# A chunked GRU with a spline layer behind it: side-by-side last input groups, a short first step, an earlier count, and extremes in eight parts

## What is computed

```python
gi = x @ W_ih + b_ih
gh = h @ W_hh + b_hh
r, z = sigmoid(i_r + h_r), sigmoid(i_z + h_z)
n = tanh(i_n + r * h_n)
h_new = (1 - z) * n + z * h
...
tok_min, tok_max = x_slice.min(axis=1), x_slice.max(axis=1)   # per token
tile_min = where(onehot, tok_min, inf).min(axis=1)            # per expert: the extremes
```

## Time and profile before

| | |
|---|---|
| median of 3 runs | 2472.63 us (2471.12 to 2473.9) |
| the profiled execution | 2474.04 us, its span 2472.5 us |
| PE busy | 2342.8 us (95%) |
| DVE busy | 1299.0 us (53%) |
| ACT busy | 658.0 us (27%) |
| POOL busy | 214.4 us (9%) |
| granted TensorE clock, mean | 0.970 |

### The profile page before, as it was taken

How to read it: one execution, slowest core, us unless ns; L and a number is a source line. 1 busy time by engine, 2 the same in 40 slices (tenths; PEclk the granted TensorE clock), 3 DMA queues, 4 the chain that set the end, 5 groups by cost and what they waited for, 6 DMA issues and landing times. The chain is left out here.

```text
span 2472.5 us, 83702 instructions
## 1 busy us (share of the span) xinstructions
PE 2342.8 (95%) x35300; PEld 1287.7 (52%) x35300; DVE 1299.0 (53%) x2691; ACT 658.0 (27%) x1333; POOL 214.4 (9%) x440
## 2 busy tenths in 40 slices
PE   7999999999999989999999999999999999977736
PEld 3444444444444445555666656666666666644412
DVE  4322121212122357676666655666666666888867
ACT  3200000000001133333333332333333333355530
POOL 0000000000000000000000000111111111123224
PEclk9999999999999999999999999999999999999965
DMA  7693131313132445444444443444444444478830
GB/s 238 204 336 128 52 128 50 126 52 128 51 145 103 153 148 156 143 143 131 136 136 136 136 132 103 120 113 117 119 115 116 119 119 119 114 221 233 240 86 5
DMA packets 177335, 330.61 MB, mean 134 GB/s; under 512 B 24272, under 2 KB 87168, under 8 KB 176192
## 3 DMA queue, kind: packets, MB, share of 16 engines
q1 hardware_dynamic: 145360, 267.53, 34.0%
q10 hardware_dynamic: 24192, 44.05, 4.8%
q0 software_dynamic: 7680, 17.57, 4.5%
HBM read 222.39 MB, written 156.77 MB: 153 GB/s over the span
## 5 line engine op out<-in xcount | busy, mean ns | idle before, releaser
L581 PE MATMUL banks<-w_hi,hi 128*32 128x512 f16 (+1 forms) x13824 | 613.1, 332 | 30.8 <-DVE hi L887 18.3
L581 PEld LDWEIGHTS banks<-w_hi,hi 128*32 128x32 f16 x13824 | 366.2, 98 | 256.9 <-issue 32.3
L314 DVE SCALAR_TENSOR_TENSOR out_stage<-acc,bias_row 128x512 f32<-128x512 f32 x168 | 116.0, 691 | 623.5 <-PE acc L372 623.5
L581 PE MATMUL banks<-w_lo,hi 128*32 128x512 f16 (+1 forms) x8192 | 355.4, 326 | 0.0
L581 PE MATMUL banks<-w_hi,lo 128*32 128x512 f16 (+1 forms) x8192 | 355.0, 326 | 0.0
L370 PE MATMUL acc<-w_hi,x_even 128*128 128x512 f16 x768 | 292.3, 381 | 12.7 <-DVE x_even L306 11.1
L371 PE MATMUL acc<-w_hi,x_even 128*128 128x512 f16 x768 | 292.2, 380 | 0.0
L372 PE MATMUL acc<-w_lo,x_even 128*128 128x512 f16 x768 | 292.1, 380 | 0.0
L581 PEld LDWEIGHTS banks<-w_lo,hi 128*32 128x32 f16 x8192 | 218.5, 97 | 114.9 <-issue 0.5
L581 PEld LDWEIGHTS banks<-w_hi,lo 128*32 128x32 f16 x8192 | 218.3, 97 | 114.5
L709 ACT ACTIVATE rz<-sums 128x512 f32<-128x512 f32 x176 | 110.9, 630 | 541.0 <-DVE sums L852 541.0
(11 more groups left out here) (172 smaller groups left out, 2167.0 us busy)
## 6 DMA issues: line engine op xcount, KB each, us to landing
stage<-gi_scratch SPq DMA_DIRECT2D x704, 96.0 KB
gi_scratch<-out_stage ACTq DMA_DIRECT2D x168, 256.0 KB, 2.0
stage<-sums_scratch SPq DMA_DIRECT2D x40, 512.0 KB
stage<-in_xT SPq DMA_DIRECT2D x32, 512.0 KB, 6.5
y<-in_x_rows SPq DMA_DIRECT2D x32, 512.0 KB, 4.4
hs_scratch<-h SPq DMA_DIRECT2D x128, 128.0 KB
x_keep<-hs_scratch SPq DMA_DIRECT2D x32, 512.0 KB, 3.9
y<-hs_scratch POOLq DMA_DIRECT2D x32, 512.0 KB, 8.2
```

Source lines behind the costliest of these rows:

```text
L314: nc.vector.scalar_tensor_tensor(out=out_stage[:, tb], in0=acc[e % BANKS][:], scalar=UNSCALE, in1=bias_row[:].rearrange("p q f -> p (q f)" ...
L581: last = nc.tensor.matmul(bank[q * COLS:(q + 1) * COLS, 0:b - a], state[:, s, j], w[:, j, q * QW + a:q * QW + b], start=first and j == 0, ...
```

## The change

- The last four groups of the last block made here (column block 5) go side by side: a quarter of k for each of the four, then the next quarter. After each quarter but the last PE counts `last_used`, and ACT and DVE convert that piece of W_hh. ACT stores the last group behind the last conversion. The clearing of the state moves ahead of the block.
- The first warm step (ZERO) multiplies one block of the state, which is zero, in place of eight. PE's first round of four steps is written out ahead of the loop.
- Set a's additional counts move to the last warm step, right behind its conversion (ACT) and its remainder (DVE); that iteration is written out on both.
- The first batch of extremes has 16 tiles, the second 14; the 15 instructions are in eight parts, and the first batch's stand in tiles 18 to 21, two in each. PE's code of these tiles is cut accordingly.

```diff
 DIFF_TILE = DIFF_FROM // 2
 
 
-EARLY = DIFF_TILE - 4
+EARLY = DIFF_TILE - 6
 ENDS_TILES = ((0, EARLY), (EARLY, TILES - 2), (TILES - 2, TILES))
 ENDS_STEPS = 15
 ENDS_MOST = max(b - a for a, b in ENDS_TILES)
...
-            for cb in range(CBLOCKS):
+            for cb in range(CBLOCKS - 1):
                 for tb in range(TB):
                     store_gi(act, EARLY_BLOCKS - 1, cb * TB + tb)
                 act.wait_ge(acc_ready, (EARLY_BLOCKS - 1) * ACCS + (cb + 1) * TB)
                 for kp in range(XPARTS):
                     split_w_hi(act, PIECES + cb * XPARTS + kp, cb * XPARTS + kp)
+            for kp in range(XPARTS):
+                if kp == XPARTS - 1:
+                    for tb in range(TB - 1):
+                        store_gi(act, EARLY_BLOCKS - 1, (CBLOCKS - 1) * TB + tb)
+                if kp < XPARTS - 1:
+                    act.wait_ge(last_used, kp + 1)
+                else:
+                    act.wait_ge(acc_ready, EARLY_BLOCKS * ACCS)
+                split_w_hi(act, 2 * PIECES - XPARTS + kp, PIECES - XPARTS + kp)
+            store_gi(act, EARLY_BLOCKS - 1, ACCS - 1)
...
+            for s in range(SETS):
+                nc.vector.memset(t["h"][:, s, 1], 0.0)
+                nc.vector.memset(t["hi"][:, s], 0.0)
+            nc.vector.memset(t["flag"][:], 1)
             for cb in range(CBLOCKS):
+                if cb == CBLOCKS - 1:
+                    for kp in range(XPARTS - 1):
+                        split_w_lo(dve, PIECES + cb * XPARTS + kp, cb * XPARTS + kp)
                 for tb in range(TB):
                     evict(dve, EARLY_BLOCKS - 1, cb * TB + tb, False)
                     if cb == 0:
                         split_x_lo(dve, EARLY_BLOCKS, 1, tb * KX)
-                for kp in range(XPARTS):
+                for kp in range(XPARTS - 1 if cb == CBLOCKS - 1 else 0, XPARTS):
                     split_w_lo(dve, PIECES + cb * XPARTS + kp, cb * XPARTS + kp)
-            for s in range(SETS):
-                nc.vector.memset(t["h"][:, s, 1], 0.0)
-                nc.vector.memset(t["hi"][:, s], 0.0)
-            nc.vector.memset(t["flag"][:], 1)
...
-                for e in range(ACCS):
+                for e in range(ACCS - TB if u else ACCS):
                     whole(EARLY_BLOCKS - 2 + u, 1 - u, e)
+            for e in range(ACCS - TB, ACCS):
+                pe.wait_ge(acc_free, (EARLY_BLOCKS - 1) * ACCS + (e + 1))
+            for kp in range(XPARTS):
+                for e in range(ACCS - TB, ACCS):
+                    last = products(0, e, range(kp * KX, (kp + 1) * KX))
+                    if kp == XPARTS - 1:
+                        last.then_inc(acc_ready, 1)
+                if kp < XPARTS - 1:
+                    last.then_inc(last_used, 1)
...
-    FULL, HEADS, KEPT, DIFFS, LAST = range(5)
+    FULL, HEADS, KEPT, DIFFS, LAST, ZERO = range(6)
...
-        def pe_products(s, w, state, first, closing):
-                for j in range(JB):
+                for j in range(blocks):
...
+                elif mode == ZERO:
+                    pe_products(s, w_hi, hi, True, True, 1)
                 else:
                     pe_products(s, w_hi, hi, mode == HEADS, True)
...
-                    pe_run(pe, cb * 2 + i // 2, i % 2, 1, HEADS)
+                    pe_run(pe, cb * 2 + i // 2, i % 2, 1, ZERO if isinstance(cb, int) and i == 0 else HEADS)
                     for k in range(i * SETS, (i + 1) * SETS):
                         pe_late(pe, cb, k)
 
-            with pe.Fori(0, CBLOCKS) as cb:
+            heads(0)
+            with pe.Fori(1, CBLOCKS) as cb:
                 heads(cb)
...
-                with pe.Fori(2, DIFF_TILE - 2 if first else TILES) as i:
+                with pe.Fori(2, DIFF_TILE - 4 if first else TILES) as i:
                     tile(i)
                 if first:
                     pe.wait_ge(rows_split, 5)
-                    tile(DIFF_TILE - 2, lambda: pe_affine(pe, 0, 0))
+                    tile(DIFF_TILE - 4, lambda: pe_affine(pe, 0, 0))
+                    with pe.Fori(DIFF_TILE - 3, DIFF_TILE - 1) as i:
+                        tile(i)
                     tile(DIFF_TILE - 1)
...
-            with act.Fori(WARM_HEADS // 2, WARM // 2) as it:
+            def kept(it, last):
                 for u in range(2):
                     for s in range(SETS):
                         act_step(act, it, u, s, 0, after_tanh=lambda: act_save(act, it, u, s))
+                        if last and (u, s) == (1, 0):
+                            act.wait_ge(hi_ready[s], WARM + 1)
+                            act.sem_inc(hi_ready[s], 1)
                         act_keep(act, it, u, s)
+            with act.Fori(WARM_HEADS // 2, WARM // 2 - 1) as it:
+                kept(it, False)
+            kept(WARM // 2 - 1, True)
...
                     if first and s == 0:
-                        act.wait_ge(hi_ready[s], WARM + 1)
-                        act.sem_inc(hi_ready[s], 1)
                         continue
...
                 step(3, nc.vector.tensor_tensor(scaled, scaled, affine[:, a:b, 0:SLICE], ALU.mult))
+            elif part == 1:
                 step(4, nc.vector.tensor_tensor(records, scaled, affine[:, a:b, SLICE:2 * SLICE], ALU.add))
                 step(5, nc.vector.tensor_reduce(low, records, AX.X, ALU.min))
                 step(6, nc.vector.tensor_reduce(high, records, AX.X, ALU.max))
-            elif part == 1:
+            elif part == 2:
                 step(7, nc.vector.tensor_scalar(miss[:, 0:n], hits[:, a:b], 0.0, BIG, ALU.is_equal, ALU.mult))
                 step(8, nc.vector.tensor_tensor(hit_ends, hits[:, a:b], of_experts(low), ALU.mult))
+            elif part == 3:
                 step(9, nc.vector.tensor_tensor(hit_ends, hit_ends, miss[:, 0:n], ALU.add))
-            elif part == 2:
+            elif part == 4:
                 step(10, nc.vector.tensor_reduce(batch_ends[:, 0], by_expert, AX.X, ALU.min))
                 step(11, nc.vector.tensor_tensor(t["ends"][:, 0], batch_ends[:, 0], t["ends"][:, 0] if batch else batch_ends[:, 0], ALU.min))
+            elif part == 5:
                 step(12, nc.vector.tensor_tensor(hit_ends, hits[:, a:b], of_experts(high), ALU.mult))
+            elif part == 6:
+                step(13, nc.vector.tensor_tensor(hit_ends, hit_ends, miss[:, 0:n], ALU.subtract))
             else:
-                step(13, nc.vector.tensor_tensor(hit_ends, hit_ends, miss[:, 0:n], ALU.subtract))
                 step(14, nc.vector.tensor_reduce(batch_ends[:, 1], by_expert, AX.X, ALU.max))
                 step(15, nc.vector.tensor_tensor(t["ends"][:, 1], batch_ends[:, 1], t["ends"][:, 1] if batch else batch_ends[:, 1], ALU.max))
...
-            with dve.Fori(WARM_HEADS // 2, WARM // 2) as it:
+            def kept(it, last):
                 for u in range(2):
                     for s in range(SETS):
                         dve_step(dve, it, u, s, 1, KEPT)
+                        if last and (u, s) == (1, 0):
+                            dve.wait_ge(lo_ready[s], WARM + 1)
+                            dve.sem_inc(lo_ready[s], 1)
+            with dve.Fori(WARM_HEADS // 2, WARM // 2 - 1) as it:
+                kept(it, False)
+            kept(WARM // 2 - 1, True)
...
                     dve.sem_inc(turned[0], 1)
-                    dve.sem_inc(lo_ready[0], 1)
                     dve.wait_ge(start_shifted, 64)
...
-                with dve.Fori(2, DIFF_TILE - 2 if first else TILES) as i:
+                with dve.Fori(2, DIFF_TILE - 4 if first else TILES) as i:
                     tile(i, (FULL, FULL), True)
                 if first:
-                    tile(DIFF_TILE - 2, (FULL, FULL), True, 0)
-                    tile(DIFF_TILE - 1, (FULL, LAST), True, 2)
+                    for k in range(3):
+                        tile(DIFF_TILE - 4 + k, (FULL, FULL), True, 2 * k)
+                    tile(DIFF_TILE - 1, (FULL, LAST), True, 6)
...
                 if not first:
-                    for part in range(4):
+                    for part in range(8):
                         dve_ends(dve, p, 0, part)
-                dve_ends(dve, p, 1, 0)
+                for part in range(2):
+                    dve_ends(dve, p, 1, part)
...
                 dve.wait_ge(gap_summed, p + 1)
                 nc.vector.tensor_copy(flag[:], misc_bank[0:1, 64:65]).then_inc(pass_judged, 1)
-                dve_ends(dve, p, 1, 1)
+                for part in range(2, 4):
+                    dve_ends(dve, p, 1, part)
                 dve_signed(dve, T)
                 dve_route(dve, T)
-                dve_ends(dve, p, 1, 2)
-                dve_ends(dve, p, 1, 3)
-                for part in range(4):
+                for part in range(4, 8):
+                    dve_ends(dve, p, 1, part)
+                for part in range(8):
                     dve_ends(dve, p, 2, part)
```

(8 more changed lines are left out.)

## The result

The changed kernel takes **2457.9 us** (median of 5 runs, 2456.71 to 2460.95) against 2472.63 (median of 5, 2470.49 to 2473.9): a ratio of 0.9942, 95% interval [0.9931, 0.9954], so 14.7 us less where 16.2 were forecast. The profiled execution took 2458.56 us, its span 2457.0 (before 2474.04 and 2472.5).

A forecast was written before the change was run, and what follows sets the result against it. PE was taken to bound the kernel except in two gaps (8.5 and 3.9 us), DVE's chain and transfers from 2165 us. Terms 4.5 + 4.8 + 5.1 + 2.3 + 0.15 - 0.6 = 16.2 us gave 2456.4 us, range 2451.5 to 2463.

The forecast's parts named there:

- Part 1: Gap ahead of the first recurrence product: last input groups side by side let PE start at 890.4, 4.5 us gained.
- Part 2: First recurrence step: a zero state needs one block of eight, step done 8.7 us after restart, not 13.49; 4.8 us gained.
- Part 3: Hand-over to the main pass: set a counted at its own step, set b starts at 1473.95, not 1479.04; 5.1 us gained.
- the lower bound: Hand-over to the main pass: only 2.5 us gained if the clock falls in the new gap.
- Part 4: Start of the difference stage: extremes in eight parts let set b's last sums start earlier; 2.3 us gained.
- The affine block: Affine products: 48 in place of 54, 0.15 us gained.
- The tail: Second batch of extremes: 14 tiles for 12 lengthen its instructions, partly covered by the wait for POOL; 0.6 us lost.
- The clock staying up in the first gap: Rival: no clock fall there, step 2 at 17.2 us, 6.9 gained for 4.8, total 2454.3; chance 0.15.
- The stage giving 2.3 us back: Rival: transfers, not its start, set the difference stage's pace, so 2.3 us are lost again; total 2458.7, chance 0.2.
- Part 3 not doing what it says: Rival at the hand-over: another count or buffer still holds set a, 5.1 us stay; total 2461.5, chance 0.07.
- Four banks in turn at half clock: Rival in the last input groups: going round four banks runs at half clock, 20.7 us more; total 2477.1, chance 0.01.
- PE's code: Rival at PE's newly laid-out loop entries: late fetches cost 4.6 us each, five make it 2479.4; chance 0.03.

The follow-up runs named there:

- 4.9 alone: Kernel before with only the last input groups put side by side; 2491.49 us, ratio 0.9976 to the kernel before.
- part 3 alone: Kernel before with only set a's additional counts moved to the last warm step; 2492.06 us, ratio 0.9986 to the kernel before.
- the first set: Runs of the kernel before with one part of the change at a time, 11 runs each; the kernel before took 2496.87 us there.
- the delays: Changed kernel with two or six additional reductions on DVE ahead of set b's last full step; 2462.03 and 2470.81 us, ratios 0.9957 and 0.9979 to the kernel before.
- the filled hand-over: Changed kernel plus 11 idle products ahead of set b's first products of the main pass; 2481.72 us, ratio 0.9945 to the kernel before.
- the split ones: Changed kernel with two of the four transfers that shift set b's starts issued by ACT, not SP; 2481.92 us, ratio 0.9945 to the kernel before.
- the first gap filled: Changed kernel plus 15 idle products behind the last input group, 2480.94 us; with 11 more at the hand-over, in another set, 2458.49 us.
- part 4 alone: Kernel before with only the extremes in eight parts; 2497.29 us, ratio 0.9999 to the kernel before.
- the second set: Changed kernel again, with either gap filled, or with the shift split, 5 runs each; unaltered it took 2484.65 us, the kernel before 2495.75.

## Why the prediction was right

The total came nearer than its terms. Against the forecast, part 1 gave 0.5 us more and part 2 gave 1.0 more, part 3 gave 2.4 less; the stage of differences, taken as neutral, gave back some 1.5, and from the beginning of the second batch on 1.0 is gained where 0.6 was to be lost. The paths of all four parts were the predicted ones; that the misses nearly cancel is luck.

- **Part 1, forecast 4.5, measured 5.0** (4.9 alone). The path was the predicted one. The term mis-sized, by 0.5 us, is the store: "which ACT now issues behind the conversion, at 887.65" was issued at 887.14, beside it.
- **Part 2, forecast 4.8, measured 5.8.** The step that missed is "it stayed there for some 5.8 us of the work", taken over from the execution before. Half clock lasted only from 0.7 to 4.1 us behind the restart here, and step 1 came after 7.7 us in place of the predicted 8.7. In two other executions of the same program half clock ended 5.6 us behind the restart and step 1 came after 8.76, just as predicted. So the 5.8 us gained are those of one pair of executions; the other pairs give 4 to 5. The states did follow: conversions at 895.42 and 899.57, 5.5 and 9.6 us behind the restart, for "5.3" and "9.5".
- **Part 3, forecast 5.1, measured 2.65 here and 4.6 alone.** Set a's products went ahead as said. Two things failed. "So b starts at 1473.95": from the turned state to the conversion that releases set b it took 1463.41 - 1456.61 = 6.80 us, where it had been 6.03, so that the wait was 2.47 us and not 1.7. And "It is shorter than the 3.3 us after which the clock fell here" was no reason for a clock that stays up: it fell all the same, some 0.2 us behind the end of that wait, and the first pass lost 1.7 us. That is the case of the lower bound, 2.5. (The 3.3 itself is 3.1: by the 0.74 of the earlier trace rows the fall lies at 1467.5, not 1467.7.) That the clock falls less surely than the sum assumed, in either way, is shown by the runs: the hand-over with part 3 alone kept it after 2.19 us.
- **Part 4, forecast 2.3, measured 2.36** at the first difference product, 2.35 at the gamma row. On the chip of the first set it is worth only 0.8 us there, and its ratio is 0.9999 [0.9990, 1.0008]. That an earlier start reaches the end is argued from the delays, which move the same place the other way; no timed run shows the 2.3 us themselves.
- **The affine block, 0.15**: the lead grew from 13.46 to 13.62 up to the products' end.
- **The tail, forecast -0.6.** The instructions grew as said (0.96 to 1.09, 1.44 to 1.65), and the wait for POOL covered the second part as said; from DVE's L1002 of the second batch to that of the third it came to 0.1 us more (20.97 to 21.07). What the forecast lacks is the 1.1 us gained behind that, in PE's wait for DVE ahead of the spline. It repeats in every profiled execution of the change (above), so it is a gain of the change that nobody forecast. The 1.6 us that the lead shrank by within the stage is another matter: the table shows that this much means nothing in a single execution.
- **The rivals.** The clock staying up in the first gap did happen, in one profiled execution with that gap unfilled (the filled hand-over: idle 3.48 us, then set a's step 1 after 6.05 us and a wait of 1.35 for set b). Its price was too high: step 2 came 18.2 us behind the restart, not 17.2, which is 0.1 us better than the first profile with its short half clock. The stage giving 2.3 us back: not borne out by the delays, which reach the end as a mean, but a part of it stays possible (above). Part 3 not doing what it says: refuted. Four banks in turn at half clock: 49 products in 10 us at a granted clock of 1.00, so what the Trainium skill (TensorE: Matmul & The Clock Gate, A second HAM failure mode: psum-queue depth-cycling) says of going round banks is not what this trace shows. It speaks of a clock that goes back and forth between its two levels, so the 20.7 us of that rival, half clock throughout, was the most that it could have cost. PE's code: no unreleased wait at an entry on this chip. The 4.6 us of the earlier trace rows are there again (4.5); that code fetched too late causes them, no run here shows.

What stays open: why the shift took 0.8 us longer than before (SP's four issues took 3.35 us for 3.82, and the split ones ended earlier without effect). From the first issue to the waiting copy it is 4.8 to 5.1 us in the four kernels without part 3 and 5.5 to 6.0 in eight of the ten executions with it, but 5.1 and 4.6 in the two with the first gap filled; so the longer landing goes with part 3, and not always. Open too is how much of 14.7 us against a ledger of 15.5 to 16.2 is scatter. The interval of the ratio, 11.4 to 17.1 us of 2472.63, holds both.

## What to carry to other kernels

Where an engine waits for a state that has long been made, ask which count holds it: a wait counted on a later step costs as much as a slow transfer, and taking it away reveals the next late one, here a small transfer that PE waits 2.5 us for. Price a gap of TensorE at its idle time plus what the clock may take behind it, as a range and not a number taken from one execution. Idle products that fill a gap hold the clock, but have a fixed length: where the awaited input comes earlier they are what the engine waits for. And before a lead that grows or shrinks in one trace is called chance or given back, compare the same stretch in all executions: here the stage scattered by 7.6 us, and the 1 us gained behind it came back every time.

## What was not expected

- **The clock's fall is not decided by the length of the gap.** At the hand-over it fell after 2.24, 2.30, 2.42, 2.47 and 2.58 us of idling (first pass 4.37 to 4.47 us) and stayed up after 2.19, 2.31 and 1.76 (2.78). In all five it fell only when PE was already at work again, 0.2 to 1.0 us behind its start. In the first gap it fell after 3.48 us in several executions (step 1 7.7 or 8.8 us behind the restart; the fall lies between 1.2 us ahead of the restart and 1.4 behind it) and did not fall after 3.48 in another (6.05). The Trainium skill (TensorE: Matmul & The Clock Gate, Part 1) says that activity is watched on a free-running window and that the number of slow products varies from run to run; the traces agree with that.
- **Chips differ more than this change is worth.** In the first two sets the kernel before took 23 to 24 us more than beside the first profile. There PE has short unreleased waits in the full tiles, 8.3 us in the kernel with part 4 alone and 8.4 in the changed one; with and without the change they are alike, which fits ratios that agree all the same. Who PE waited for, 1170 to 2140 us, changed kernel of the second set:
```profile
PE banks L605 <- issue: 8.4, 37, 0.4
```
In the first profiles, before and after, there is no such row. From set b's first products to the products' end it takes 2176.05 - 1465.34 = 710.7 us there for 2151.13 - 1463.88 = 687.3, so 23.5 of the 28.2 us between these two spans lie in the full tiles. The records show 8.4 of them as idle time; what the rest is, and what causes it, stays open. What an edit is worth differs with it: part 4's 2.35 us became 0.8.
